# K and V projections of the context attention in the two column halves of TensorE's array

## The reference

```python
k_dca = _ln(kv_dca[:, :, 0], kn_dca_w, kn_dca_b)      # the last 16 context rows, apart
q = _ln((x @ Wq + bq).reshape(b, s1, H, HD), qn_w, qn_b)
kv = jnp.concatenate([y_main @ Wk + bk, y_main @ Wv + bv], axis=-1)
k = _ln(kv[..., :HD], kn_w, kn_b)                      # H = 16 heads of HD = 32
v = kv[..., HD:]
ctx = _attn(qT, k.transpose(0, 2, 1, 3), v.transpose(0, 2, 1, 3))   # softmax(q k) v
return (ctx + ctx_dca) @ Wo + bo
```

## Time and profile before

| | |
|---|---|
| median of 3 runs | 3083.88 us (3082.59 to 3091.93) |
| the profiled execution | 3080.41 us |
| its span, first to last instruction | 3078.6 us |
| busy: TensorE, VectorE, ScalarE, GpSimd | 91%, 84%, 74%, 52% |
| instructions in the span | 94131 |
| mean granted TensorE clock | 0.960 of full speed |

### The profile page before, as it was taken

One profiled execution on the slowest core, in us unless ns is written; L12 is line 12 of the kernel. 1 busy time (PEld: TensorE's weight loads), 2 busy tenths in 40 slices (PEclk: granted clock), 3 DMA queues, 4 the chain that ended last, 5 costly groups with the idle time before them and its releaser, 6 DMA issues. The chain is left out here.

```text
span 3078.6 us, 94131 instructions
## 1 busy us (share of the span) xinstructions
PE 2816.6 (91%) x37417; PEld 1666.0 (54%) x37417; DVE 2570.9 (84%) x4146; ACT 2272.8 (74%) x4155; POOL 1615.3 (52%) x2006
## 2 busy tenths in 40 slices
PE   7689999999999778789996779999999999968889
PEld 3245555555555556577773325555555555545646
DVE  6699999999999656768875679999999999957752
ACT  6479999999999854446664458999999999964431
POOL 1257777777777643212223326777777777752200
PEclk9899999999999889899998899999999999979989
DMA  3345554555554244349895345545555555430020
GB/s 126 95 87 87 97 84 89 94 87 86 94 89 82 56 158 151 133 167 299 301 304 150 104 85 94 90 86 92 90 85 94 88 87 93 73 93 1 1 75 28
DMA packets 542717, 328.93 MB, mean 107 GB/s; under 512 B 459381, under 2 KB 504565, under 8 KB 536522
## 3 DMA queue, kind: packets, MB, share of 16 engines
q1 hardware_dynamic: 534314, 295.63, 43.2%
q0 software_dynamic: 7680, 25.17, 2.8%
q10 hardware_dynamic: 288, 2.10, 0.2%
HBM read 181.86 MB, written 36.09 MB: 71 GB/s over the span
## 5 line engine op out<-in xcount | busy, mean ns | idle before, releaser
L335 POOL TENSOR_TENSOR a_elo<-a_e 128x1024 f16<-128x1024 f32 x428 | 856.5, 2001 | 285.6 <-ACT a_e L422 285.6
L590 PE MATMUL a_ps_k<-l_wk,a_yh 128*128 128x512 f16 (+1 forms) x1664 | 571.3, 384 | 32.5 <-POOL a_yl L317 22.0
L590 PE MATMUL a_ps_v<-l_wv,a_yh 128*128 128x512 f16 (+1 forms) x1664 | 567.8, 382 | 17.9 <-DVE a_v L482 16.9
L493 DVE TENSOR_REDUCE a_mx<-a_ps_m 128x2 f32<-128x1024 f32 x384 | 467.7, 1218 | 20.3 <-PE a_ps_m L616 20.0
L420 ACT ACTIVATE a_e<-a_ps_t 128x1024 f32<-128x1024 f32 x428 | 409.3, 956 | 42.4 <-PE a_ps_t L650 39.9
L422 ACT ACTIVATE a_e<-a_ps_t 128x1024 f16<-128x1024 f32 x428 | 410.5, 959 | 0.0
L650 PE MATMUL a_ps_t<-a_qb,a_kk 64*128 64x128 f16 (+1 forms) x9672 | 351.0, 219 | 8.9 <-ACT a_e L422 8.3
L650 PEld LDWEIGHTS a_ps_t<-a_qb,a_kk 64*128 64x128 f16 (+1 forms) x9672 | 281.6, 96 | 122.8 <-issue 90.7
L590 PE MATMUL a_ps_k<-l_wk,a_yl 128*128 128x512 f16 (+1 forms) x832 | 318.4, 383 | 0.0
L452 DVE SCALAR_TENSOR_TENSOR a_kc<-a_ps_k,l_bk 128x512 f32<-128x512 f32 (+1 forms) x416 | 283.2, 681 | 41.4 <-PE a_ps_k L590 40.2
L590 PE MATMUL a_ps_v<-l_wv,a_yl 128*128 128x512 f16 (+1 forms) x832 | 315.9, 380 | 0.0
(11 more groups left out here) (415 smaller groups left out, 5283.9 us busy)
## 6 DMA issues: line engine op xcount, KB each, us to landing
l_land<-in_ctx SPq DMA_DIRECT2D x96, 384.0 KB, 3.9
l_ob<-in_m_w SPq DMA_DIRECT2D x32, 1024.0 KB, 8.0
f_w<-in_m_w SPq DMA_DIRECT2D x32, 512.0 KB, 4.8
eo_dram<-f_e_eo SPq DMA_DIRECT2D x32, 512.0 KB, 4.5
l_land<-in_ctx SPq DMA_DIRECT2D x32, 433.0 KB, 4.0
a_kk<-a_khl SPq DMA_TRANSPOSE x416, 3.1
qs_dram<-p_q SPq DMA_DIRECT2D x32, 128.0 KB, 2.3
dca_dram<-p_od SPq DMA_DIRECT2D x16, 256.0 KB, 2.4
```

The lines of the kernel that those rows point to most:

```text
L335: pool.tensor_tensor(rest[0:r, :, 0:w], full[0:r, :, 0:w], high[0:r, :, 0:w], ALU.subtract)\
L493: dve.tensor_reduce(mx[:, g, :, c], ps_m[:, :, :], AX.X, ALU.max).then_inc(mx_done, 1)
L590: m = pe.matmul(out[0:r, :], part[:, n % 2, c, cols], w[:, wpart, c, :], start=(c == 0 and a == 0), stop=(c == KC - 1 and a == 2))
```

## The change

A full projection tile is no longer one product with 128 context rows in the array's columns but two products of 64 context rows, the first in columns 0 to 63 and the second in columns 64 to 127, with the same moving weights; each writes its own 64 partitions of `ps_k` or `ps_v`. Tile 12, with 49 rows, has one product as before. In `out` the sum of both parts is written back into PSUM in place of `osum`, and the last step reads it there.

```diff
@@ out, on VectorE
                     dve.wait_ge(os_done, 2 * n + 1)
-                    dve.tensor_tensor(osum, o3[:, :, 0:HD], osum, ALU.add).then_inc(os_done, 1)
+                    dve.tensor_tensor(o3[:, :, 0:HD], o3[:, :, 0:HD], osum, ALU.add).then_inc(os_done, 1)
                     dve.wait_ge(rl_done, n + 1)
                     dve.wait_ge(os_done, 2 * n + 2)
-                    dve.tensor_tensor(osum, osum, rl[:, half, :].unsqueeze(2).broadcast_to([P, 4, HD]), ALU.mult)\
+                    dve.tensor_tensor(osum, o3[:, :, 0:HD], rl[:, half, :].unsqueeze(2).broadcast_to([P, 4, HD]), ALU.mult)\
                        .then_inc(o_done, 1)
@@ project, on TensorE
                     pe.wait_ge(yl_done, n + 1)
-                    cols = slice((i - c * PER) * P, (i - c * PER) * P + r)
                     steps = [(yh, 0), (yl, 0), (yh, 1)]
+                    o = (i - c * PER) * P
                     for c in range(KC):
                         for a, (part, wpart) in enumerate(steps):
-                            m = pe.matmul(out[0:r, :], part[:, n % 2, c, cols], w[:, wpart, c, :],
-                                          start=(c == 0 and a == 0), stop=(c == KC - 1 and a == 2))
+                            for half in range(0, r, 64):
+                                h = min(64, r - half)
+                                m = pe.matmul(out[half:half + h, :], part[:, n % 2, c, o + half:o + half + h], w[:, wpart, c, :],
+                                              start=(c == 0 and a == 0), stop=(c == KC - 1 and a == 2))
                     m.then_inc(done, 1)
```

## The result

| | before | after |
|---|---|---|
| median | 3084.47 us (4 runs, 3082.59 to 3091.93) | 3056.91 us (4 runs, 3055.45 to 3062.12) |
| ratio after / before | | 0.9916, 95% interval 0.9902 to 0.9930 |
| profiled span | 3078.6 us | 3056.3 us |
| turn of the context attention | 57.99 us | 57.0 us |

The account below looks back on a forecast made before the run. TensorE sets the pace, VectorE 1.1 us behind per 57.99 us turn. 3080.4 - 32.0 (shape changes) + 5.1 + 1.4 (lost in waits) = 3054.9; with 3.5 from profiled run to median 3058.4, said as 3058, range 3046 to 3082.

Parts of the forecast that it names:

- the price of an edge: On TensorE in the context attentions, each change of the array's shape between consecutive products costs about 0.092 us.
- 350 edges: Shape changes removed from TensorE's order, 175 in each of two layers, saving 32.0 us in all.
- Pairs at the price of one product: In full K and V projections, two 64-column products cost the 0.216 us of one, nothing added, for 4,608 pairs.
- the 3 ns of the scores: Extra per close pair seen in score products; if it held for projection pairs, 14 us in all, time 3072.
- Weight loads: Two 64-column loads per projection pair, 114 ns each, hidden beside each other or under the stream; cost 0.
- Losses in the waits: TensorE's waits before unit 8's values and V tile 4 lose 0.093 and 0.088 us a turn, 5.1 us over 28 turns.
- the 0.05 taken for the rest: Loss per turn in us where VectorE comes close elsewhere, 1.4 us in all; bound half of the gain.
- Output sums at 0: VectorE's second output step writing PSUM and third reading it, 64 times, changes the time by -0.3 to +0.3 us; taken as 0.
- The partners: Rival: VectorE and loops through ScalarE and GpSimd take over, leaving a third of the gain, 3074 us; chance 0.12.
- The loads: Rival: a projection pair's two weight loads run one after the other, 12 ns per pair, 55 us, time 3113; chance 0.06.
- the halves are not serial: Rival denied here: a projection's column halves run serially, 995 us more, about 4,080 us; chance 0.02.
- the cost goes with the shape and not with the product: Rival denied here: edge loss comes from changing product, not array shape, so no effect, 3084 us; chance 0.06.

Follow-up runs that it names:

- K or V alone: Only K, or only V, projected in column halves, the other whole, sums as in the changed kernel; ratio to the kernel before 1.0029 for K, 0.9995 for V.
- the halves alone: Changed kernel with projections in column halves but output sum and last step back in SBUF; median 3063.9 us, ratio 0.9928 to the kernel before.
- the kernel that has nothing else: Kernel before with only the output sums moved to PSUM, projections whole; median 3080.6 us, ratio 0.9981 to the kernel before.

## Why the prediction was right

*What bounds, and the price of an edge.* Right. The loss goes with the array's shape. I had 0.092 us per edge; the gaps themselves fell by 0.09 to 0.10, and the first step inside the new shape is also shorter (the second value pair 0.03 instead of 0.05 after the first, V's second product 0.22 instead of 0.23), so an edge is worth 0.10 to 0.12. Against that, each entry into a halved projection from another shape costs about 0.01 more, first gap 0.24 instead of 0.23. Neither was in the sum.

*350 edges.* Right by count: the traces have 175 fewer in each layer. The kernels with K or V alone confirm the counting, K in sign and size, V as no difference; by single turns V alone stands a few hundredths above what its one edge less would give.

*Pairs at the price of one product.* Right, 0.216 us, apart from the first pair after another shape; L1382 was the row to go by, and not the 3 ns of the scores. (L1382's own first pair was slower too, which the prediction saw and left out.) *Weight loads.* Right: 0.11 each, hidden.

*Losses in the waits.* 0.87 us per turn was forecast for the edges less 0.23 lost, and the halves alone gave 0.89. V4 lost its edge as said, unit 8's values start 0.11 later after the maxima in the halves alone (0.09 forecast), and the 0.05 taken for the rest is near the loss at V6. In the 68 stretches of a turn, the halves alone are shorter than the kernel before by 1.21 us in all and longer by 0.31: that 0.11, and 0.20 that is mostly the slower entries into halved projections. So the total is right by terms that offset each other: edges worth more than forecast against entries that the sum had at nothing.

*Output sums at 0, with 0.3 us either way.* This is the term that was mis-sized: 0.10 us in every turn, 2.8 us in all over 28 turns, 4.8 over the 15 distances of L503 in both layers (their last ones are not full turns and scatter), and 5.9 us by the ratio of the kernel that has nothing else (2.2 to 9.3). The step that failed is that I priced only VectorE's own durations, equal at 292 ns, and did not ask what GpSimd was reading meanwhile, although the stretched 2.23 us stood in the earlier trace rows and the view of L531 had a longest of 825 ns beside its median of 292.

*Rivals.* The partners do not bind the changed kernel: VectorE's load is no bound, single loops through ScalarE, GpSimd and VectorE take parts of the gain. The loads are hidden, the halves are not serial, and the cost goes with the shape and not with the product. That 3058 came so near to 3056.9 is partly luck: the halves alone, all that the forecast counted, are at 0.9928 of the kernel before, which is 3062 (3057 to 3068), and the sums, priced at nothing, made up the rest.

## What to carry to other kernels

On a TensorE that sets the pace, count how often consecutive products change the rows-by-columns shape of the array, and give neighbouring steps one shape; splitting a product in two halves costs next to nothing here when the halves alternate (0.01 us for each entry from another shape), but halving only one of two adjacent kinds adds edges. Where GpSimd streams from SBUF at the same time, keep one input of a VectorE step in PSUM: here that was worth 0.10 us a turn. Before exchanging steps to save more on the busiest engine, look for the next loop that it waits in: what is saved inside such a loop is waited away.

## What the runs showed of the hardware

- A change of the array's shape costs about 0.093 us between streams (0.309 us from start to start instead of 0.216), and the first gap after it is 0.01 to 0.02 us longer.
- Products of one column half can pass waiting products of the other half that stand before them in the list: here the seventh started before the fourth. The Trainium skill, "TensorE: Matmul & The Clock Gate", section Part 3 (The mechanism), has matmuls strictly in order in start and end; the starts at 604.799 and 605.009 us speak against it for column halves, and the measurement decides.
- A VectorE step with two SBUF inputs that meets a GpSimd difference lasted 2.22 us instead of 0.29; one that was already running stretched GpSimd's from 2.13 to 2.23. With the sum in PSUM neither happened in 64 steps.
